# A new order of steps, codes cast by DMAs, and outer-product tables in a two-layer block kernel

## The chip, the core and the metric

One core of a Trainium2 chip runs the program. The time is that of one execution in device microseconds, smaller is better; the median of three runs of the kernel before is 320.33 us (320.06 to 322.46). TensorE (PE) multiplies matrices into eight banks of PSUM; VectorE (DVE), ScalarE (ACT) and GpSimd (POOL) work on tiles; SyncE (SP) issues DMAs. Each engine goes through its own queue in program order and waits on semaphores.

## What is computed

1,024 tokens of width 512 (four sequences of 256) go through two layers, each a normalization and two branches that are added to the input. Cut to what matters:

```python
xn = layernorm(x)                                   # layer 0
h = xn @ Win.T + bin                                # width 64
for l in range(4):
    y = silu(layernorm(h, ln1))
    h = h + scl * real(conv(y, p ** t))             # complex recurrence over a sequence
    y = layernorm(h, ln2)
    h = h + silu(y @ W1.T + b1) @ W2.T + b2
attn = layernorm(h) @ Wout.T + bout
ffn = (silu(xn @ (gate_t * gate_s).T) * (xn @ (up_t * up_s).T)) @ (down_t * down_s).T   # codes -1, 0, 1; width 1792
x = x + attn + ffn
xn = layernorm(x)                                   # layer 1
attn = xn @ (weight * blockmask).T + bias
ffn = low-rank gated layer: U1, V1 (1376 wide), U2, V2
x = x + attn + ffn
```

## The kernel before

The tokens are two blocks `b` of 512, each four tiles `t` of 128. `build_order` makes one list of steps, and every engine walks this list and does its share of each step; so a place in the list is a place in all queues. The backbone are dense steps: `gate` and `up` of 14 column blocks `f` (8 matmuls of 512 columns each: high and low half of the tokens, `xh` and `xl`, times the codes, lines 628 and 629), then 16 `down` quarters (line 723) for each block. In layer 1 follow `u1`, eleven `hidden` pieces, `attn` and `out`. Each dense step is a slot, and small steps are put behind a slot.

The small steps are: `stats`, `root`, `norm`, `xt` (statistics on DVE, the inverse root on POOL at line 1104, the scaled tile XN on DVE at line 927, its transpose on PE at line 590, the copies xh and XT on ACT, the low half `xl` on DVE at line 933); the chain of the 64-wide branch, for each block `win`, and for each depth `t1`, `scan`, `z`, `scale`, `t3`, `low`, `w1`, `w2`, each with a small normalization `ln` that goes PE, ACT (square, line 830), DVE (sum and variance, lines 970 and 971), POOL (root), DVE (`scale`, line 981), PE; the `cast` steps. The places come from distances: `CHAIN_START`, and LN_SLOTS, SCAN_SLOTS and the like from step to step.

Codes are int32 in memory. SP loads each 128x512 block of them into one of six places of `stage`, and ACT (line 816, all `down` and some `up`) or DVE (line 1010) casts it to f16. A place is loaded again when its cast is done. `first` is the pair `gate` 0, `up` 0, done tile by tile as the tokens come; pair 1 waits for all four tiles. Gated products go ACT silu (line 857), DVE `hid` (line 1041), ACT `hidh` (line 789), POOL `hidl` (line 1162), with three buffers.

The recurrence uses tables `rot` of the powers of a unit complex number, 4 depths by 256 powers. They grow by doubling, eight `grow` steps of four instructions (lines 528 and 530): six on POOL, two on DVE, and then `lower` copies half of them (line 964).

The lines that place the sequence of casts read:

```python
after[up_at(0, f) - 1].append(("cast", "gate", f + 2))
after[up_at(0, f)].append(("cast", "up", f + 2))
after[up_at(0, f)].append(("cast", "down", f))
```

## Time and profile before

| | |
|---|---|
| median of the runs | 320.33 us |
| the profiled execution, and its span | 320.86 us, 319.0 us |
| PE, PEld busy | 289.1, 188.6 us |
| DVE, ACT, POOL busy | 203.1, 127.6, 151.8 us |
| PE waits for DVE `XN`, in total | 13.5 us in 4 waits |
| PE waits for DVE `lno`, `ymini`, `hid` | 3.6, 3.1, 2.1 us |
| chain that ended last: PE, DVE, POOL | 68%, 15%, 7% |
| loads of codes, 42 of 256 KB, issue to landing | 2.9 to 3.1 us |

Usual instructions: the ACT copy of a transposed tile 0.60 us, the ACT cast 0.62, silu 0.69, DVE `xl` 0.69, tile statistics 0.69 + 0.18 + 0.15, XN 0.55, `hid` 0.75, the DVE cast of codes 0.43, DVE sums of squares 0.42, `scale` 0.69, a 128x256 product on DVE 0.42, the centring of `rows` and `win` 19.24 to 22.40 us, POOL `hidl` 1.16 to 1.47.

The span goes from the first to the last instruction. Matmul ends are modelled, so a matmul's length says less than the time from start to start. Idle time of an engine matters where another waits for it.

### The profile page before, as it was taken

The numbers are of one execution on the slowest core, as the hardware profiler recorded it, in microseconds if no ns is written. First come the engines' busy times: TensorE is split into PE (matmuls) and PEld (weight loads), VectorE is DVE, ScalarE is ACT, GpSimd is POOL, SyncE is SP. The second block draws the span as 40 slices with busy tenths as digits, with TensorE's granted clock in tenths as the row PEclk, the third lists the DMA queues.
The fourth block names the chain that finished last, engine by engine and source line by source line (L and its number), as shares of the span: only waits on it lengthen the run. The fifth ranks groups of instructions, "written<-read, shape, count | busy, mean of one in ns | idle before, by whom it ended". The sixth has DMA issues, their size and how long they took to land.

```text
span 319.0 us, 4327 instructions
## 1 busy us (share of the span) xinstructions
PE 289.1 (91%) x1514; PEld 188.6 (59%) x1514; DVE 203.1 (64%) x316; ACT 127.6 (40%) x213; POOL 151.8 (48%) x161
## 2 busy tenths in 40 slices
PE   0859596989999999999999999996999999999995
PEld 0737253746456564656456464553658888888784
DVE  3679899998764758556675654578977751333313
ACT  1563363555663313254553626212114671045610
POOL 3476452869625220236534444616066893029920
PEclk9999798999999999999999999999999999999999
DMA  7947333645531001301010011110001000110003
GB/s 215 325 150 260 104 106 93 197 129 170 165 132 35 6 26 35 99 0 47 7 33 20 33 35 34 35 31 2 1 8 61 0 0 2 66 66 2 0 1 132
DMA packets 12261, 22.84 MB, mean 72 GB/s; under 512 B 1360, under 2 KB 1872, under 8 KB 12240
## 3 DMA queue, kind: packets, MB, share of 16 engines
q1 hardware_dynamic: 12240, 22.57, 22.2%
q8 instruction: 12, 0.20, 0.2%
q14 instruction: 9, 0.07, 0.1%
HBM read 20.46 MB, written 2.10 MB: 71 GB/s over the span
## 4 chain that ended last, share of the span: by engine, by line
PE 68%; DVE 15%; POOL 7%; issue 4%; ACT 3%; DMA 1%; SPq 0%; DVEq 0%; ACTq 0%; POOLq 0%
PE bank L723 11%; PE bank L628 9%; PE bank L629 9%; PE bank L598 8%; PE bank L596 8%; PE bank L597 8%; PE bank L683 4%; POOL root L1104 3%; PE bank L590 2%; POOL hidl L1162 2%; DVE uscan L999 2%; PE bank L661 2%; POOL X L1150 2%; PE bank L655 1%; DMA X<-in_x 1%
## 5 line engine op out<-in xcount | busy, mean ns | idle before, releaser
L1162 POOL TENSOR_TENSOR hidl<-hid,hidh 128x512 f16<-128x512 f32 x28 | 34.0, 1214 | 62.5 <-ACT hidh L789 62.5
L628 PE MATMUL bank<-xh,upw 128*128 128x512 f16 (+1 forms) x124 | 44.7, 371 | 2.4 <-DVE hid L1041 2.1
L628 PE MATMUL bank<-xh,gatew 128*128 128x512 f16 (+1 forms) x124 | 44.7, 371 | 1.7 <-DVE xl L933 1.4
L629 PE MATMUL bank<-xl,upw 128*128 128x512 f16 (+1 forms) x124 | 44.8, 371 | 0.0
L629 PE MATMUL bank<-xl,gatew 128*128 128x512 f16 (+1 forms) x124 | 44.5, 369 | 0.0
L723 PE MATMUL bank<-downw,hidh 128*128 128x512 f16 x112 | 42.5, 379 | 0.0
L723 PE MATMUL bank<-downw,hidl 128*128 128x512 f16 x112 | 42.4, 379 | 0.0
L1104 POOL TENSOR_TENSOR root<-var,powers 128x4 f32<-128x4 f32 (+1 forms) x25 | 24.9, 996 | 35.1 <-DVE var L971 26.4
L1168 POOL TENSOR_TENSOR actl<-hid,acth 128x512 fp32r<-128x512 f32 (+1 forms) x22 | 28.4, 1300 | 22.7 <-ACT acth L796 22.2
L857 ACT ACTIVATE silu<-bank,early 128x512 f32<-128x512 f32 x28 | 19.2, 687 | 32.3 <-PE bank L629 32.3
L1041 DVE SCALAR_TENSOR_TENSOR hid<-bank,early,silu 128x512 f32<-128x512 f32 x28 | 21.0, 750 | 13.9 <-PE bank L629 13.0
L1072 DVE SCALAR_TENSOR_TENSOR hid<-bank,early,silu 128x512 f32<-128x512 f32 (+1 forms) x22 | 16.5, 750 | 17.8 <-ACT silu L872 14.5
L872 ACT ACTIVATE silu<-bank,early 128x512 f32<-128x512 f32 (+1 forms) x22 | 15.1, 688 | 26.6 <-PE bank L598 26.6
L590 PE MATMUL bank<-early,XN 128*128 128x128 f32 x64 | 11.9, 319 | 13.5 <-DVE XN L927 13.5
L628 PEld LDWEIGHTS bank<-xh,upw 128*128 128x128 f16 x124 | 13.0, 105 | 15.0 <-DVE hid L1041 2.6
L970 DVE TENSOR_REDUCE ssum<-lno 128x4 f32<-128x256 f32 x18 | 7.6, 420 | 21.6 <-ACT lno L830 21.4
L628 PEld LDWEIGHTS bank<-xh,gatew 128*128 128x128 f16 x124 | 13.0, 105 | 13.9 <-DVE xl L933 1.9
L789 ACT ACTIVATE hidh<-hid 128x512 f16<-128x512 f32 x28 | 17.4, 622 | 7.9 <-DVE hid L1041 7.9
L830 ACT ACTIVATE lno<-bank 128x256 f32<-128x256 f32 x18 | 6.9, 381 | 34.2 <-PE bank L683 18.3
L629 PEld LDWEIGHTS bank<-xl,upw 128*128 128x128 f16 x124 | 12.7, 102 | 11.2 <-issue 0.7
L629 PEld LDWEIGHTS bank<-xl,gatew 128*128 128x128 f16 x124 | 12.7, 102 | 10.9 <-issue 0.5
L590 PEld LDWEIGHTS bank<-early,XN 128*128 128x128 f32 x64 | 9.2, 166 | 16.7 <-issue 14.4
(145 smaller groups left out, 640.4 us busy)
## 6 DMA issues: line engine op xcount, KB each, us to landing
stage<-in_gate SPq DMA_DIRECT2D x14, 256.0 KB, 3.1
stage<-in_up SPq DMA_DIRECT2D x14, 256.0 KB, 2.9
stage<-in_down SPq DMA_DIRECT2D x14, 256.0 KB, 2.9
X<-in_x SPq DMA_DIRECT2D x8, 256.0 KB, 6.5
out_x<-X SPq DMA_DIRECT2D x8, 256.0 KB, 2.0
stage<-in_v SPq DMA_DIRECT2D x6, 256.0 KB, 2.6
stage<-in_mask SPq DMA_DIRECT2D x4, 256.0 KB, 3.0
stage<-in_weight SPq DMA_DIRECT2D x4, 256.0 KB, 2.6
```

The source lines that it names most:

```text
L590: mm = pe.transpose(bank_of(key)[:, k * P:(k + 1) * P], XN[:, key[2], k * P:(k + 1) * P], ident)
L596: pe.matmul(dst, lhs[0], rhs[0], start=first, stop=False)
L597: pe.matmul(dst, lhs[0], rhs[1], start=False, stop=False)
L598: return pe.matmul(dst, lhs[1], rhs[0], start=False, stop=last)
L628: pe.matmul(bank_of(key)[:, c], w, xh[b][:, k, c], start=(k == 0), stop=False)
L629: mm = pe.matmul(bank_of(key)[:, c], w, xl[b][:, k, c], start=False, stop=(k == KT - 1))
L723: mm = pe.matmul(bank_of(key)[:], part[:, f, t * P:(t + 1) * P], codes["down"][:, f, :], start=(f == 0 and part is hidh), stop=(f == FT - ...
L857: act.activation(silu[:, n % UNITS, :], bank_of(step)[:], ACT.Silu, scale=col("gate_s", f)).then_inc(silu_ready, 1)
L1041: emit(dve.scalar_tensor_tensor(out=hid[:, n % UNITS, :], in0=bank_of(step)[:], scalar=col("up_s", f), in1=silu[:, n % UNITS, :], op0=ALU. ...
L1104: pool.tensor_tensor(root[i][:, t:t + n], var[i][:, t:t + n], powers[:, 0, t:t + n], ALU.pow).then_inc(root_ready[i], 1)
L1162: pool.tensor_tensor(hidl[:, n % FT, :], hid[:, n % UNITS, :], hidh[:, n % FT, :], ALU.subtract).then_inc(hid_lo, 1)
L1168: pool.tensor_tensor(actl[0:K, n % UNITS, :], hid[0:K, n % UNITS, :], acth[0:K, n % UNITS, :].bitcast(F32), ALU.subtract).then_inc(hid_lo, 1)
```

## The change

The order becomes a table: each small step has a slot of its own, with decimals for its rank within the slot (`LN_AT`, `CHAIN_AT` and so on), and the prologue is written out as `PROLOGUE`. The dense steps keep their order but for `attn` and `u1` in layer 1.

- Only `gate` and `up` 0 and 1 go through `stage` and are cast by ACT. All other codes are loaded by six DMAs of POOL that cast from int32 to f16 on the way, straight into the code tiles; PE waits for the semaphore of the whole load. `stage` has five places. SP's queue is shorter by 38 loads; `early` is loaded by ACT's queue.
- The first two pairs are done tile by tile; four banks hold them, and transposes of tiles 2 and 3 take the two banks of `h`.
- The tables: POOL makes 16 fine and 16 coarse powers (eight `grow` steps of three instructions), `turn` copies them to `turned`, and each depth's table is an outer product, two multiplications and an addition of 128x256: depth 0 on DVE, 1 to 3 on POOL.
- The copy XT is a step of its own, `xcopy`, and the bank of a transpose is free only behind it; `xl` reads the bank and no longer XT.
- The square goes to a tile `sq` with a column for epsilon, and one reduction makes the variance.
- `u1` writes its low half to a tile of its own, `plow`. The casts of `w` no longer wait for the last `wo`. ACT loads its silu table at the start. WARM is 0: PE does nothing ahead of the first tokens, as before.

```diff
-NSTAGE = 6
+FIRST_LOADS = 4
+NSTAGE = 5
...
-CHAIN_START = (3, 12)
-LN_SLOTS, SCAN_SLOTS = 2, 3.3
...
+PROLOGUE = ((("seed", 0), ("stats", 0), ("stats", 1), ("norm", 0), ("seed", 1), ("norm", 1), ("stats", 2)),
+            (("xt", 0), ("codes", 0), ("load", 0), ("norm", 2), ("seed", 2), ("stats", 3), ("grow", 0)),
+            (("xt", 1), ("codes", 1), ("first", 0, 0), ("norm", 3), ("load", 1), ("grow", 1)),
+            (("xt", 2), ("first", 0, 1), ("xcopy", 0), ("first", 1, 0), ("grow", 2), ("grow", 3)),
+            (("xt", 3), ("first", 1, 1), ("xcopy", 1), ("first", 2, 0), ("first", 2, 1), ("xcopy", 2),
+             ("first", 3, 0), ("first", 3, 1), ("xcopy", 3)))
+EARLY_GROWTHS = 4
+WARM = 0
...
+CODE_LOADS = (("gate", 2, 6), ("up", 2, 6), ("gate", 6, 14), ("up", 6, 14), ("down", 0, 7), ("down", 7, 14))
+LOAD_AT = (0.2, 0, 7.1, 16.2)
+GROW_AT = (0, 0, 0.1, 0.5, 0.5, 0.5)
+LN_AT = (0.1, 1.1, 1.2, 1.4, 1.7, 4.1, 4.4, 5.0, 6.4)
+TABLE_AT = (5.3, 7.8, 8.1, 13.3)
+XT_AT = (4.5, 6.6, 8.9, 9.3)
+XCOPY_AT = (7.5, 8.0, 9.1, 9.9)
...
-def cast_by_act(kind, i):
-
-    return kind == "down" or i == 0 or (kind == "up" and 1 < i < ACT_UPS)
...
+        if kind == "xt" and step[1] == 0 and step[2] >= 2:
+            take(step, RING + step[2] - 2)
...
-        ph, pl = xs
+        ph, pl = xs[0], plow[:]
...
-                "xt": lambda: (xt_hi, at),
+                "xt": lambda: (xt_copied, at),
...
+            for i, (kind, first, end) in enumerate(CODE_LOADS):
+                if kind == cast[0] and first <= cast[1] < end:
+                    eng.wait_ge(codes_in[i], 16)
...
-        def growth(eng, i, part):
-
-
-
-            n = 1 << i
-            known, grown, other = rot[:, :, :, 1:n + 1], rot[:, :, :, n + 1:2 * n + 1], rot_t[:, :, :, 0:n]
-            if part < 2:
-                nth = rot[:, :, part:part + 1, n:n + 1].to_broadcast([P, DEPTH, 2, n])
-                return eng.tensor_tensor(other if part else grown, known, nth, ALU.mult)
-            c = part - 2
-            return eng.tensor_tensor(grown[:, :, c, :], grown[:, :, c, :], other[:, :, 1 - c, :],
-                                     ALU.add if c else ALU.subtract)
...
+        def outer(eng, l, part, work):
+
+
+
+            n = [P, ROOTN, ROOTN]
+            dst = rot[:, l, :].rearrange("p (a c) -> p a c", a=ROOTN)
+            tmp_ = rot_t[:, work, :].rearrange("p (a c) -> p a c", a=ROOTN)
+            if part == 2:
+                return eng.tensor_tensor(dst, dst, tmp_, ALU.add)
+            return eng.tensor_tensor(tmp_ if part else dst, turned[:, part, l, :].unsqueeze(2).to_broadcast(n),
...
-                            for by in codes_ready:
-                                pe.wait_ge(codes_ready[by], len(ternary[by]))
...
+            act.dma_start(early[:], params).then_inc(prm_in, 16)
+            act.wait_ge(pool_chain, 1)
+            act.activation(warm[:], powers[:, 0, 0:1], ACT.Silu)
...
-                    if b == 1 and t == 0:
-                        act.wait_ge(h_full[0], 1)
-                        act.wait_ge(xt_lo, TPB)
                     wait_full(act, step)
                     src = bank_of(step)[:].rearrange("p (k n) -> p k n", k=KT)
                     c = slice(t * P, (t + 1) * P)
-                    act.activation(xh[b][:, :, c], src, ACT.Copy)
-                    act.activation(XT[:, :, c], src, ACT.Copy).then_inc(xt_hi, 1)
+                    act.activation(xh[b][:, :, c], src, ACT.Copy).then_inc(xt_hi, 1)
+                elif kind == "xcopy":
+                    _, b, t = step
+                    if b == 1 and t == 0:
+                        act.wait_ge(h_full[0], 1)
+                    act.wait_ge(xt_lo, b * TPB + t + 1)
+                    src = bank_of(("xt", b, t))[:].rearrange("p (k n) -> p k n", k=KT)
+                    act.activation(XT[:, :, t * P:(t + 1) * P], src, ACT.Copy).then_inc(xt_copied, 1)
...
-                    act.activation(lno[b][:, :, 0:DIM], h[b], ACT.Square).then_inc(sq_ready[b], 1)
+                    act.activation(sq[b][:, :, 0:DIM], h[b], ACT.Square, scale=DIM ** -0.5).then_inc(sq_ready[b], 1)
...
-                    emit(dve.tensor_reduce(ssum[b][:], lno[b][:, :, 0:DIM], AX.X, ALU.add))
-                    emit(dve.tensor_scalar(var[b][:], ssum[b][:], 1.0 / DIM, EPS, ALU.mult, ALU.add),
-                         var_ready[b])
+                    emit(dve.tensor_reduce(var[b][:], sq[b][:], AX.X, ALU.add), var_ready[b])
...
-                            if i == 0:
-                                wait_full(dve, ("wo", 1, TPB - 1))
...
+                    half, i = divmod(step[1], GROWTHS // 2)
+                    table, n = (fine, coarse)[half], 1 << i
+                    if half == 1 and i == 0:
+                        link(pool.tensor_copy(coarse[:, :, 1, :], fine[:, :, ROOTN, :]))
+                    both = [P, DEPTH, 2, 2 * n]
+                    known = table[:, :, 1:n + 1, :].rearrange("p l t c -> p l (t c)").unsqueeze(2).to_broadcast(both)
+                    nth = table[:, :, n, :].unsqueeze(3).to_broadcast(both)
+                    link(pool.tensor_tensor(prod[:, :, :, 0:n, :].rearrange("p l a t c -> p l a (t c)"),
+                                            known, nth, ALU.mult))
+                    link(pool.tensor_tensor(table[:, :, n + 1:2 * n + 1, 0], prod[:, :, 0, 0:n, 0],
+                                            prod[:, :, 1, 0:n, 1], ALU.subtract))
+                    link(pool.tensor_tensor(table[:, :, n + 1:2 * n + 1, 1], prod[:, :, 0, 0:n, 1],
+                                            prod[:, :, 1, 0:n, 0], ALU.add))
...
+                elif kind == "table" and step[1] > 0:
+
+                    for part in range(2):
+                        link(outer(pool, step[1], part, 1))
+                    outer(pool, step[1], 2, 1).then_inc(table_ready, 1)
+                    pool.wait_ge(table_ready, step[1])
+                elif kind == "load":
+                    what, first, end = CODE_LOADS[step[1]]
+                    pool.dma_start(codes[what][:, first:end, :],
+                                   source[what][first:end].rearrange("f p d -> p f d")).then_inc(
+                                       codes_in[step[1]], 16)
```

**VectorE, behind the last `xl` of the prologue.** `hid` is the gated product of a pair, `st`, `mv`, `var` the statistics of a tile of the second block, `gatew` a cast, `rot` and `yff` the growth of the tables, XN the scaled tiles. Before:

```order
L1010 CAST gatew<-stage 128x512
L911 BN_STATS st<-X 128x6
L912 BN_AGGR mv<-st 128x2
L1041 SCALAR_TENSOR_TENSOR hid<-bank,early,silu 128x512
L911 BN_STATS st<-X 128x6
L912 BN_AGGR mv<-st 128x2
L911 BN_STATS st<-X 128x6
L912 BN_AGGR mv<-st 128x2
L915 TENSOR_SCALAR var<-mv 128x4
L528 TENSOR_TENSOR rot<-rot 128x8x64
L528 TENSOR_TENSOR yff<-rot 128x8x64
L530 TENSOR_TENSOR rot<-rot,yff 128x4x64 x2
```

After:

```order
L1011 SCALAR_TENSOR_TENSOR hid<-bank,early,silu 128x512
L885 BN_STATS st<-X 128x6
L886 BN_AGGR mv<-st 128x2
L885 BN_STATS st<-X 128x6
L886 BN_AGGR mv<-st 128x2
L885 BN_STATS st<-X 128x6
L886 BN_AGGR mv<-st 128x2
L889 TENSOR_SCALAR var<-mv 128x4
L942 TENSOR_REDUCE var<-sq 128x4
L1011 SCALAR_TENSOR_TENSOR hid<-bank,early,silu 128x512
L901 TENSOR_SCALAR XN<-X,mv,root 128x512 x2
L908 TENSOR_TENSOR xl<-bank,xh 128x4x128
```

The `hid` of the upper list is that of pair 1; the lower list begins with pair 0, and pair 1 is its tenth row. The casts among the statistics and the growth behind the variance are gone; `hid` 1 stands behind all statistics and behind the first sum of squares (`var<-sq`), where it stood in their middle.

**GpSimd, from the last growth to the first `hidl` and roots.** Before:

```order
L528 TENSOR_TENSOR rot<-rot 128x8x32
L528 TENSOR_TENSOR yff<-rot 128x8x32
L530 TENSOR_TENSOR rot<-rot,yff 128x4x32 x2
L1162 TENSOR_TENSOR hidl<-hid,hidh 128x512 x2
L1104 TENSOR_TENSOR root<-var,powers 128x4 x2
L1162 TENSOR_TENSOR hidl<-hid,hidh 128x512
L1183 TENSOR_TENSOR W1l<-stage,W1h 128x512
L1162 TENSOR_TENSOR hidl<-hid,hidh 128x512
```

After, where the casting loads stand between growth instructions (two places), and then the end of the tables:

```order
L1120 TENSOR_TENSOR fine<-prod 128x4x8
L1137 DMA upw<-in_up 128x8x512
L1112 COPY coarse<-fine 128x4x2
L1116 TENSOR_TENSOR prod<-coarse 128x8x2
```

```order
L1120 TENSOR_TENSOR coarse<-prod 128x4x4
L1137 DMA gatew<-in_gate 128x8x512
L1116 TENSOR_TENSOR prod<-coarse 128x128
```

```order
L1124 COPY turned<-coarse 64x64
L1125 TENSOR_SCALAR turned<-coarse 64x64
L1126 COPY turned<-coarse 64x64
L1127 COPY turned<-coarse 64x64
L1162 TENSOR_TENSOR hidl<-hid,hidh 128x512
L1079 TENSOR_TENSOR root<-var,powers 128x4 x2
L1162 TENSOR_TENSOR hidl<-hid,hidh 128x512 x2
L1183 TENSOR_TENSOR W1l<-stage,W1h 128x512
L1162 TENSOR_TENSOR hidl<-hid,hidh 128x512
L1137 DMA downw<-in_down 128x7x512
L497 TENSOR_TENSOR rot<-turned,fine 128x256
L497 TENSOR_TENSOR rot_t<-turned,fine 128x256
```

Four DMAs of POOL have come in ahead of the first `hidl`, two of them with 128x8x512 elements; the 128x256 growth is gone, `turned` has come, and the tables of depths 1 and 2 follow behind the third `hidl`, with the load of `down`.

**SyncE, behind the prologue's loads.** Before:

```order
L567 DMA tmp<-in_rows 128x320
L568 DMA late<-in_params 128x960
L570 DMA X<-in_x 128x512 x4
L561 DMA stage<-in_gate 128x512
L561 DMA stage<-in_up 128x512
L561 DMA stage<-in_down 128x512
```

After:

```order
L532 DMA tmp<-in_rows 128x320
L533 DMA late<-in_params 128x960
L535 DMA X<-in_x 128x512 x4
L526 DMA stage<-in_wide 128x512
L538 DMA bc<-in_rows 128x1024
L526 DMA stage<-in_wide 128x512 x2
L526 DMA stage<-in_mask 128x512 x4
```

The loads of codes are gone from it; what is left goes through five places.

## Rows read from the trace of the kernel before

**Rows 1.** Stages: stretch, its us, busy us (instructions) of PE, PEld, DVE, ACT, POOL, clock, DMA.

```profile
25.50:62.10 36.60, 29.56 (x167) 18.71 (x166) 34.37 (x50) 14.80 (x27) 18.46 (x19) 0.91 0.46 144
62.10:120.00 57.90, 56.27 (x310) 32.59 (x310) 40.33 (x61) 26.91 (x46) 29.16 (x24) 1.00 0.31 98
120.00:200.00 80.00, 78.03 (x426) 45.04 (x425) 49.73 (x76) 36.43 (x60) 31.35 (x28) 1.00 0.12 34
200.00:233.00 33.00, 29.68 (x152) 17.55 (x150) 26.41 (x45) 5.59 (x9) 12.66 (x11) 1.00 0.06 17
233.00:315.60 82.60, 82.60 (x370) 65.36 (x368) 35.57 (x52) 31.68 (x52) 45.52 (x37) 1.00 0.06 21
```

**Rows 2.** Timeline of PE: start us, us, engine, line, what [idle before <-releaser].

```profile
7.94 1.08 PE L590 MATMUL bank<-early,XN 128*128 128x128 f32 x4 [7.94 <-DVE XN L927]
...
11.08 0.31 PE L629 MATMUL bank<-xl,gatew 128*128 128x128 f16 x1
11.19 0.31 PE L628 MATMUL bank<-xh,gatew 128*128 128x128 f16 x1
...
23.70 0.39 PE L628 MATMUL bank<-xh,upw 128*128 128x512 f16 x1 [2.06 <-DVE hid L1041]
...
25.22 0.38 PE L629 MATMUL bank<-xl,upw 128*128 128x512 f16 x1
...
36.57 1.09 PE L590 MATMUL bank<-early,XN 128*128 128x128 f32 x4 [3.88 <-DVE XN L927]
...
51.99 1.10 PE L661 MATMUL bank<-late,ymini 128*128 128x64 f32 x8 [3.05 <-DVE ymini L1002]
...
58.62 3.68 PE L646 MATMUL bank<-late,XT 128*128 128x64 f32 x32
62.14 0.38 PE L628 MATMUL bank<-xh,upw 128*128 128x512 f16 x1
...
223.18 0.47 PE L693 MATMUL bank<-Wouth,xs 128*128 128x512 f32 x1 [1.61 <-issue]
```

**Rows 3.** Stages as in rows 1, the two behind the long pauses.

```profile
36.20:39.60 3.40, 3.03 (x10) 1.62 (x11) 2.63 (x4) 1.08 (x2) 0.00 (x0) 0.50 0.35 131
53.30:56.70 3.40, 3.40 (x12) 1.70 (x10) 3.23 (x6) 1.42 (x3) 0.75 (x1) 0.50 0.27 84
```

**Rows 4.** 17.5 to 61.6 us of lines 1010, 528, 530 alone (two: DVE, then POOL).

```profile
17.50:61.60 44.10, 6.34 (x11) 0.92 0.45 142
...
17.50:61.60 44.10, 4.61 (x4) 4.74 (x12) 0.92 0.45 142
...
17.50:61.60 44.10, 2.54 (x4) 3.59 (x12) 0.92 0.45 142
```

**Rows 5.** Timeline of DVE, columns as in rows 2.

```profile
6.11 0.69 DVE L911 BATCH_NORM_STATS2 st<-X 128x6 f32<-128x512 f32 x1 [1.54 <-DMA X<-in_x]
...
40.42 0.43 DVE L1010 CAST gatew<-stage 128x512 f16<-128x512 int32 x1
...
42.07 1.39 DVE L1029 CAST W1h<-stage 128x512 fp32r<-128x512 f32 x1
```

**Rows 6.** 18.8 to 28.9 us of POOL alone, the growth of before.

```profile
18.80:28.90 10.10, 8.22 (x24) 1.00 0.59 170
```

**Rows 7.** Timeline of POOL.

```profile
4.71 1.02 POOL L1117 TENSOR_TENSOR pz<-pz,powers 128x4 f32<-128x4 f32 x1
...
28.96 1.16 POOL L1162 TENSOR_TENSOR hidl<-hid,hidh 128x512 f16<-128x512 f32 x1
...
33.39 2.66 POOL L1104 TENSOR_TENSOR root<-var,powers 128x4 f32<-128x4 f32 x2
```

**Rows 8.** Timeline of SP's own DMA queue.

```profile
3.04 0.43 SPq L561 DMA_DIRECT2D stage<-in_gate  x1
```

**Rows 9.** Stage in which the loads run densest; last two: DMA share, GB/s.

```profile
12.00:14.00 2.00, 1.67 (x13) 1.62 (x13) 1.88 (x4) 0.31 (x1) 1.68 (x4) 1.00 1.04 404
```

More of the change, by code:

```diff
@@ L85, with dense_order @@
 U2_CHUNKS = chunks_of(IT * RANK)
[L88 to L116 removed]
+def dense_order():
+    dense = []
@@ new lines, in dense_order, with chain, norm_big @@
+    return dense
+def chain(b):
+    jobs = [[("win", b), ("ln", b)], [("scale", b)]]
+    for l in range(DEPTH):
+        jobs += [[("t1", b, l)], [("scan", b, l)], [("z", b, l), ("ln", b)], [("scale", b)], [("t3", b, l)],
+                 [("low", b)], [("w1", b, l)], [("w2", b, l), ("ln", b)], [("scale", b)]]
+    return jobs + [[("tf", b)], [("low", b)], [("wo", b, 0), ("wo", b, 1)], [("wo", b, 2), ("wo", b, 3)]]
+def norm_big(layer, b):
+    return ([[("stats", layer, b, t)] for t in range(TPB)] + [[("root", layer, b, 0, TPB)]]
+            + [[("norm", layer, b, t)] for t in range(TPB)])
@@ L302, in two_layers @@
     casts = [s[1:] for s in order if s[0] == "cast"]
-    ternary = {e: [c for c in casts if c[0] in ("gate", "up", "down") and (cast_by_act(*c) == (e == "act"))]
+    ternary = {e: [c for c in casts if c[0] in ("gate", "up") and e == "act"]
                for e in ("act", "dve")}
@@ L630, in gate_up @@
                 return mm
+            pe.wait_ge(ones_ready, 1)
+            for _ in range(WARM):
+                pe.matmul(banks[0][:], onesr[:], onesr[:, 0:1].to_broadcast([P, D]), start=True, stop=True)
             pe.wait_ge(prm_in, 16)
```

325 lines of the change are left out of this document (143 added, 182 removed).

## The prediction

> **What bounds the kernel now.** I read the page's engine shares first: TensorE is busy 289.1 of 319.0 us, so it carries the kernel and all that can be won is its idle time and its slow time. A table of stages then says where that lies. From 233.0 to 315.6 us it is never idle; from 62.1 to 233 it idles 1.63 + 1.97 + 3.32 = 6.9 us in short pieces; behind the last matmul come 3.4 us of adding and storing [rows 1]. From 25.5 to 62.1 it is idle 36.6 - 29.6 = 7.0 us [rows 1]. Before its first instruction stand 7.94 us, and the pieces behind it are seen one by one in its timeline: 2.06 us before the second `up` block, 3.88 us before the transpose at 36.57 (waiting for VectorE's normalized tile) and 3.05 us before `z` at 51.99 (waiting for the scan on VectorE) [rows 2]. Behind each of the two long pauses the granted clock reads 0.50 for 3.4 us, that is 1.2 in place of 2.4 GHz [rows 3]; behind the 2.06 us pause 128x512 matmuls go on at (25.22 - 23.70)/7 = 0.22 us from start to start, which is full speed [rows 2]. Two stretches of 3.4 us at half speed cost up to 1.7 us each.
>
> In the same stretch VectorE is nearly full: 34.4 of 36.6 us [rows 1]. So early on VectorE's queue sets the pace, and from 62 us on TensorE does. My mark for the early part is the start of `up` block 6 behind the second `win`: 62.14 us [rows 2].
>
> **Part 1, VectorE's load.** Between 17.5 and 61.6 us VectorE casts codes 11 times (6.34 us) and grows the tables (4.61 + 2.54 us) [rows 4]: 13.5 us. All of it goes. What comes are three 256-element products for table 0, at 0.42 each (the duration of the 128x256 `rot` instructions of before), 1.3 us; the `TENSOR_SCALAR` behind each block's sum of squares also goes. If VectorE alone set the pace, the mark would move up about 12 us.
>
> **Part 2, the first tokens, walked.** The walk takes its durations from the trace (the table of usual instructions above has those without a row): a transposed tile 1.1 us at the low clock and 0.45 at the high, 16 matmuls of 128 columns at 0.11 us each [rows 2] cold = 1.7 and 0.9 warm, copies 0.6, `xl` 0.7, statistics of a tile 1.1, normalization 0.55. Normalized tile 0 waits behind the statistics of tile 1, whose X lands at 6.11 [rows 5]; the parameters no longer stand ahead of it in SP's queue, worth at most the 0.4 us that one issue takes [rows 8]. The first transpose thus comes at 7.4 (7.94 before). TensorE then does tile 0 of pair 0 at 10.5, tile 1 of pair 0 and tile 0 of pair 1 until 16.4, tile 3's transpose at 16.8, and the rest of both pairs until 21.2. Before, pair 1 ended at 25.4 [rows 2]. The number of columns is the same: 64 matmuls of 128 in place of 16 of 512. Splitting is not free where the clock is low, but these are waits anyway.
>
> `win` needs the centred rows and weights: 3.0 us on VectorE behind `xl` of tile 3 and one tile's statistics, so it runs 22.2 to 26.0. `hid` 0 is made at 22.9, then three statistics, the variance and `hid` 1 until 27.7. Next in VectorE's queue stands the normalization of the second block, which needs GpSimd's root.
>
> **Part 3, GpSimd, the term I am least sure of.** Ahead of `hidl` 0 and that root GpSimd now has, behind the last root of the prologue at 13.1: 24 growth instructions and a copy. The 24 of before took 10.1 us with their gaps for larger outputs [rows 6]; the smaller ones I put at 9.2. Four for `scan`, 1.9; four for `turned`, 1.2; three DMA issues. One more issue stands before the prologue's last root. Behind these stand `hidl`, 1.2, and the root, which two of them in 2.66 bound by 1.3; I use 1.3 and 1.0 [rows 7].
> An issue by GpSimd has no row here. Low bound: SP's issue, 0.43 us [rows 8]. High bound: SP's 0.43 for 128 rows of 2 KB scaled by the rows, 1.7 for 512 and 3.4 for 1,024. I take 1.0, nearer to the low one, since SP's own issue does not show a price by row. The power of eight columns costs 1.0 to 2.0, from 1.02 for four [rows 7]; I take 1.65, which the walk holds. Sum: 13.1 + 9.2 + 1.9 + 1.2 + 3.0 = 28.4, root at 30.7. VectorE is ready at 27.7 and waits 3.0 us; TensorE, done with `gate` 2 at 27.5, waits 3.2 us for the transpose.
>
> From there: `up` 2 to 32.9, `gate` 3, second transpose, `up` 3 to 36.8, `t1` to 37.3, a wait of 1.4 us for ScalarE's late copy of XT (the bank of the first transpose is freed only by it, and it is queued behind `t1`'s `ymini`), `gate` 4, two transposes, `up` 4, `gate` 5 to 44.8. The scan is ready by 43, so `z` no longer waits. `up` 5, `gate` 6, `win` until 52.6. The pause of 3.2 us is like the 3.05 us one that let the clock fall [rows 2, 3]: I add 1.0 (0 to 1.7). The mark is at 53.6: **8.5 us** gained. Bounds: with TensorE never waiting behind 21.2, its work up to the mark is 26.3 us (two `win` at 3.8, nine blocks at 1.73, four transposes and `t1` at 0.45, `z` 0.84), so 47.5 and 14.6 us gained; with the dear issues (0.7 + 5.5 us more) 59.8 and 2.3 us.
>
> **Part 4, after the mark.** Of the 6.9 us the pieces of 0.56 us stand before `t1` and `t3`, whose `scale` waits behind GpSimd's 1.2 us `hidl`; the largest, 1.61 us, before `Wout` at 223.18 [rows 2]. The new table gives the links more room, 3 to 5 places from `z` to `t3` where all had 3, the reduction makes the variance itself, and VectorE loses two or three casts in the 62 to 120 us stretch. I leave 1.5 us: **5.4 us** gained, bounds 0.5 and 6.6. The later `u1` of block 1 has a copy and a subtraction (1.5 us) under 1.4 us of `out`: 0.1. The first hidden pieces lose the `attn` between them, but four pieces at 1.43 us cover the 3.6 us from gate to `actl`. TensorE's work, 289 us, does not change: in the stretch without idle nothing can be won. ScalarE's casts go too; its queue was no bound, since it is idle more than half of the time in each stage from 25.5 us on [rows 1].
>
> Sum: 319.0 - 8.5 - 5.4 = 305.1 us of span. The profiled execution took 320.86 for a span of 319.0, so 1.86 around it: 307.0; the median of the runs shown is 0.5 lower, so **306.4 us**.
>
> **A rule against this change.** VectorE's casts and GpSimd's work disturb each other here: a 128x512 cast takes 0.43 alone, and one of the same size took 1.39 while GpSimd was in a `hidl` [rows 5]. If an issue waits for one such cast, that is 0.4 us each, 1.3 us for three: the sum would be 307.7. The Trainium skill ("SBUF — State Buffer", the "DVE blocks DMA" trap) says that a DMA issued from GpSimd is starved of descriptors while VectorE runs a two-port instruction. By that rule 307.7 would be the better number; no run here shows a load issued by GpSimd. The new prologue leaves VectorE a single cast between 13 and 28 us, that of the rows, so I keep the sum.
>
> **Rivals.**
> - *Forecast* (0.50): the sum, 303.5 to 309.5.
> - *TensorE hardly waits* (0.22): an issue costs 0.4 and GpSimd is ready when VectorE is; mark at 48 to 50, 0.5 to 1 us idle later: 319.0 - 13.1 - 6.1 + 1.3 = 301.1 (1.3 from span to median).
> - *Issues hold GpSimd long* (0.13): 3.4 us for the large ones. Mark at 59.8, and 4.5 us idle later, since the late loads for `down` stand in the same queue: 319.0 - 2.3 - 2.4 + 1.3 = 315.6.
> - *New waits eat the gain* (0.07): the late XT copies, the stage with five places in place of six, and the masked weights, which make GpSimd wait for a landing, bring new gaps of some 10 us: 316 to 322, no change.
> - *Slower: the casting transfers are slow* (0.08). Each load has one semaphore, so `gate` 6 waits for the whole 2 MB, and 6 MB must have landed before `up` 6. Issued from 10 us on, they may last until 61 without making the mark later than before: 6 MB in 51 us, 123 GB/s. Plain loads run at 404 GB/s here [rows 9], and 3.3 times slower is what it takes. At 75 GB/s they end at about 94: 319 + 32 = 351 us. For it: no row shows a casting transfer. Against it: the margin.
>
> **How the numbers follow.** Over 1% faster is below 317.1: forecast, TensorE hardly waits, long issues, and a little of the new waits: 0.86. Within 1%: 0.06. Slower: 0.08. (1% is about what a measurement of this kernel tells from no change.) The range, 300.5 to 315, takes the first two cases and the lower part of the third; left out are its upper part (0.04) and the last two, 0.19 in all.
>
> **What would show it.** The first transpose at 7.4 and the second pair's last 128-column matmul near 21; VectorE waiting for `root` before the second block's `XN` near 28; GpSimd's time between the prologue's last root and the first `hidl`, 15.3 us; `z` of block 0 without a wait; `up` 6 at 53.6; idle of TensorE behind it under 2 us. I am wrong if loads land after 25.5 (TensorE waiting for DMA), or if idle behind the mark stays at 7 us.

## The result, and the profile after

The changed kernel takes 305.9 us (median of four runs, 305.4 to 307.0) beside 320.2 us for the kernel before, timed with it: a ratio of 0.954, 95% interval 0.949 to 0.959. 306.4 us was predicted, with 300.5 to 315 as the range. The profiled execution took 306.1 us with a span of 304.2, against 319.0 before.

Stages of the changed kernel, columns as in [rows 1]; the first goes from the end of the first `win` to the mark, the start of `up` 6:

```profile
24.90:54.60 29.70, 24.29 (x136) 14.37 (x136) 19.34 (x28) 11.58 (x21) 18.91 (x26) 0.94 0.65 113
54.60:112.00 57.40, 57.40 (x321) 33.99 (x319) 34.75 (x47) 23.83 (x39) 33.61 (x29) 1.00 0.16 31
112.00:192.00 80.00, 80.00 (x436) 46.43 (x434) 46.40 (x68) 37.07 (x61) 36.23 (x33) 1.00 0.10 28
192.00:225.00 33.00, 32.22 (x165) 19.34 (x165) 27.53 (x50) 5.65 (x11) 11.43 (x11) 1.00 0.11 36
225.00:304.20 79.20, 75.73 (x337) 60.99 (x335) 31.22 (x44) 30.38 (x50) 41.92 (x33) 1.00 0.08 29
```

Set beside [rows 1], VectorE is no longer full in the first stage (19.3 of 29.7 us, where it was 34.4 of 36.6), and behind the mark TensorE idles 0.8 us, where it idled 6.9. (The 3.5 us in the last stage are the adding and storing behind the last matmul, as before.) TensorE's timeline, columns as in [rows 2]; these are all of its rows with a wait:

```profile
7.31 1.94 PE L555 MATMUL bank<-early,XN 128*128 128x128 f32 x8 [7.31 <-DVE XN L901]
9.94 0.29 PE L593 MATMUL bank<-xh,gatew 128*128 128x128 f16 x1 [0.70 <-DVE xl L908]
...
20.07 0.22 PE L594 MATMUL bank<-xl,upw 128*128 128x128 f16 x1
21.19 0.36 PE L584 MATMUL bank<-rowhl,onesr 128*128 128x256 f32 x1 [0.90 <-DVE late L871]
...
24.90 0.38 PE L593 MATMUL bank<-xh,gatew 128*128 128x512 f16 x1
...
30.84 0.63 PE L555 MATMUL bank<-early,XN 128*128 128x128 f32 x4 [4.05 <-DVE XN L901]
...
40.56 0.39 PE L593 MATMUL bank<-xh,gatew 128*128 128x512 f16 x1 [1.36 <-ACT XT L785]
...
46.63 1.00 PE L630 MATMUL bank<-late,ymini 128*128 128x64 f32 x8
...
54.55 0.38 PE L593 MATMUL bank<-xh,upw 128*128 128x512 f16 x1
...
201.85 0.63 PE L624 MATMUL bank<-early,lno 128*128 128x128 f32 x4 [0.78 <-DVE lno L951]
```

The mark fell from 62.14 [rows 2] to 54.55, 7.6 us, and from the mark to the end the span fell from 256.9 to 249.65, 7.2 us. Together that is the 14.8 us by which the span fell (the medians differ by 14.3). The 3.05 us wait before `z` [rows 2] is gone; one pause of 4.05 us is left. The chain that ended last shows what made it (start, us, what; the longest pieces of its early part):

```profile
9.67 1.12 POOL gatew L1137
13.89 0.84 POOL upw L1137
18.04 0.96 POOL upw L1137
22.72 0.95 POOL gatew L1137
27.48 1.15 POOL hidl L1162
28.64 1.02 POOL root L1079
```

GpSimd's four issues of casting loads (the DMAs that turn int32 codes into f16 on the way; the issue is the time for which GpSimd is held), then `hidl` 0, then the root that the second block's normalization waits for. VectorE's timeline has the other end of it, where XN waits for that root:

```profile
26.07 0.75 DVE L1011 SCALAR_TENSOR_TENSOR hid<-bank,early,silu 128x512 f32<-128x512 f32 x1
30.15 1.89 DVE L901 TENSOR_SCALAR XN<-X,mv,root 128x512 f32<-128x512 f32 x2 [3.33 <-POOL root L1079]
```

### The profile page after: what moved, and what is told of

It reads as the page before. It is cut to its first block, busy times and chain, and to the rows that moved or that the text cites. A ratio compares the mean times of both kernels' runs of the same rounds, so it can differ in the third digit from the quotient of the medians.

```text
span 304.2 us, 4356 instructions
## 1 busy us (share of the span) xinstructions
PE 285.6 (94%) x1562; PEld 190.5 (63%) x1562; DVE 175.6 (58%) x270; ACT 118.4 (39%) x197; POOL 159.5 (52%) x184
## 4 chain that ended last, share of the span: by engine, by line
PE 85%; POOL 6%; DVE 4%; issue 2%; DMA 1%; ACT 1%; DVEq 0%; POOLq 0%
PE bank L593 15%; PE bank L594 15%; PE bank L690 14%; PE bank L561 8%; PE bank L563 8%; PE bank L562 8%; PE bank L652 5%; PE bank L624 3%; PE bank L630 2%; PE bank L555 2%; PE bank L642 1%; PE bank L643 1%; DMA early<-in_params 1%; PE bank L615 1%; POOL root L1079 1%
## 5 line engine op out<-in xcount | busy, mean ns | idle before, releaser
L594 PE MATMUL bank<-xl,upw 128*128 128x512 f16 (+1 forms) x136 | 45.7, 354 | 0.0
L1079 POOL TENSOR_TENSOR root<-var,powers 128x4 f32<-128x4 f32 (+1 forms) x25 | 23.6, 948 | 23.5 <-DVE var L942 19.8
L593 PEld LDWEIGHTS bank<-xh,gatew 128*128 128x128 f16 x136 | 14.0, 103 | 13.8 <-ACT XT L785 1.6
L845 ACT ACTIVATE silu<-bank,early 128x512 f32<-128x512 f32 (+1 forms) x22 | 15.1, 687 | 19.0 <-PE bank L563 18.8
L593 PEld LDWEIGHTS bank<-xh,upw 128*128 128x128 f16 x136 | 14.2, 105 | 11.8 <-issue 1.1
L555 PE MATMUL bank<-early,XN 128*128 128x128 f32 x64 | 10.7, 301 | 11.4 <-DVE XN L901 11.4
L594 PEld LDWEIGHTS bank<-xl,upw 128*128 128x128 f16 x136 | 13.9, 102 | 11.5 <-issue 0.8
L594 PEld LDWEIGHTS bank<-xl,gatew 128*128 128x128 f16 x136 | 13.9, 102 | 10.8 <-issue 0.3
L942 DVE TENSOR_REDUCE var<-sq 128x4 f32<-128x260 f32 x18 | 7.6, 424 | 20.4 <-ACT sq L803 20.3
L690 PEld LDWEIGHTS bank<-downw,hidh 128*128 128x128 f16 x112 | 11.2, 100 | 12.8 <-issue 1.6
L561 PE MATMUL bank<-xs,V1h 128*128 128x512 f32 (+1 forms) x44 | 18.0, 409 | 0.1
## 6 DMA issues: line engine op xcount, KB each, us to landing
upw<-in_up POOLq DMA_DIRECT2D x1, 1024.0 KB, 12.1
```

The source lines that it names most:

```text
L561: pe.matmul(dst, lhs[0], rhs[0], start=first, stop=False)
L593: pe.matmul(bank_of(key)[:, c], w, xh[b][:, k, c], start=(k == 0), stop=False)
L594: mm = pe.matmul(bank_of(key)[:, c], w, xl[b][:, k, c], start=False, stop=(k == KT - 1))
L690: mm = pe.matmul(bank_of(key)[:], part[:, f, t * P:(t + 1) * P], codes["down"][:, f, :], start=(f == 0 and part is hidh), stop=(f == FT - ...
L1079: pool.tensor_tensor(root[i][:, t:t + n], var[i][:, t:t + n], powers[:, 0, t:t + n], ALU.pow).then_inc(root_ready[i], 1)
```

## The experiments

Twelve kernels ran; each ratio is to the kernel before in the same batch, whose median went from 320.2 to 321.6 us. The changed kernel was timed in a batch of its own, so a difference from it reads a little otherwise by the ratios than by the medians; below, both are given where it matters. Spans and marks are those of the profiled executions.

| kernel | median us | ratio to before | 95% interval | span | mark |
|---|---|---|---|---|---|
| changed kernel | 305.9 | 0.954 | 0.949 to 0.959 | 304.2 | 54.55 |
| root_first | 303.0 | 0.943 | 0.940 to 0.946 | 301.6 | 51.97 |
| old_chain | 311.0 | 0.969 | 0.964 to 0.973 | 308.2 | 52.43 |
| casts_back | 309.8 | 0.963 | 0.959 to 0.967 | 306.6 | 54.85 |
| first_one | 305.8 | 0.951 | 0.948 to 0.954 | 304.0 | 54.36 |
| split_loads | 308.3 | 0.960 | 0.958 to 0.963 | 306.8 | 57.11 |
| xcopy_early | 304.9 | 0.951 | 0.948 to 0.953 | 302.9 | 53.26 |
| warm12 | 305.9 | 0.953 | 0.951 to 0.955 | 303.5 | 53.84 |
| root_xcopy_table | 302.6, again 302.5 | 0.943, 0.943 | 0.941 to 0.944 | 300.9, 300.6 | 51.24, 50.98 |
| scan_early | 306.6 | 0.955 | 0.950 to 0.960 | 305.2 | 50.10 |
| before_room | 318.0 | 0.993 | 0.990 to 0.995 | 316.0 | 61.05 |
| scan_w1 | 308.0 | 0.960 | 0.957 to 0.962 | 306.3 | 48.08 |

**GpSimd's queue.** Does it set the long pause? root_first puts the last growth step, the four `scan` products and the four `turned` copies behind the root (3.8 us of GpSimd's time in the changed kernel), and the load of `gate` 6 to 13 behind the first `hidl`:

```diff
-LOAD_AT = (0.2, 0, 7.1, 16.2)
-GROW_AT = (0, 0, 0.1, 0.5, 0.5, 0.5)
+LOAD_AT = (1.3, 0, 7.1, 16.2)
+GROW_AT = (0, 0, 0.1, 2.5, 2.5, 2.5)
```

> Only the order of GpSimd's queue changes, against the changed kernel (305.9 us): the last growth, the four scan products and the four `turned` copies go behind the roots of the second block, and the load of `gate` 6 to 13 goes behind the first `hidl`. Theory (GpSimd's queue sets the 4.05 us pause of TensorE at 30.84): the statistics of the block are ready at 24.9, the root at about 26.0, XN behind `hid` 1 at 26.8, the transpose at 27.5; the pause is 1 us and the granted clock does not fall, so the kernel gains 3.3 + 1.5 us: about 301, and the two levels of the clock show by whether the gain is 3 or 5. Rival (the pause would only move, because the scan on VectorE at 43.0 or the copies of XT then hold the next steps): less than 1.5 us gained, with a new wait before `z` or `gate` 4.

303.0 us, 2.9 us faster (3.6 by the ratios), where about 301 was expected. The root began at 25.67 and TensorE's pause shrank to 0.77 us; the granted clock stayed at 1.00. What was not expected is the first of these two waits; the second was there before:

```profile
35.99 0.63 PE L624 MATMUL bank<-early,lno 128*128 128x128 f32 x4 [1.52 <-DVE lno L951]
...
37.98 0.39 PE L593 MATMUL bank<-xh,gatew 128*128 128x512 f16 x1 [1.36 <-ACT XT L785]
```

VectorE's and then GpSimd's timeline of the same kernel say why `lno` was late:

```profile
32.08 1.26 DVE L497 TENSOR_TENSOR rot<-turned,fine 128x256 f32<-128x256 f32 x1
33.27 0.41 DVE L497 TENSOR_TENSOR rot_t<-turned,fine 128x256 f32<-128x256 f32 x1
33.72 1.40 DVE L496 TENSOR_TENSOR rot<-rot,rot_t 128x256 f32<-128x256 f32 x1
```

```profile
31.83 1.23 POOL L1162 TENSOR_TENSOR hidl<-hid,hidh 128x512 f16<-128x512 f32 x1
33.69 1.15 POOL L1162 TENSOR_TENSOR hidl<-hid,hidh 128x512 f16<-128x512 f32 x1 [0.63 <-ACT hidh L756]
```

Of three equal products of table 0, the two that met a `hidl` took 1.26 and 1.40 us, the one between them 0.41; both long ones ended 0.28 us behind the `hidl` beside them. In the changed kernel, with GpSimd idle, they took 0.42 or 0.43. So the theory on the pause holds; but the growth behind the root held `hidl` 1 back (31.83 for 30.60) until VectorE made its table.

**The price of an issue.** split_loads makes two issues of each casting load, each with half of the rows (both on the load's semaphore, whose waits go from 16 to 32):

```diff
-                    pool.dma_start(codes[what][:, first:end, :],
-                                   source[what][first:end].rearrange("f p d -> p f d")).then_inc(
-                                       codes_in[step[1]], 16)
+                    mid = (first + end) // 2
+                    for a, z in ((first, mid), (mid, end)):
+                        pool.dma_start(codes[what][:, a:z, :],
+                                       source[what][a:z].rearrange("f p d -> p f d")).then_inc(
+                                           codes_in[step[1]], 16)
```

> The changed kernel (305.9 us) with each of the six casting loads issued in two halves, so twelve issues of 256 or 512 rows (448 for `down`). Four of the added issues... of the six added, one stands ahead of the prologue's last root and three behind it ahead of the root of the second block. Theory (an issue costs GpSimd about 0.95 us whatever its rows, 0.84 to 1.14 in the changed kernel, and its queue sets XN of the second block): each half costs 0.9 to 1, the XN comes 3 to 4 us later than 30.8, the kernel takes 309 to 310. Rival A (the cost goes with the rows): a half costs 0.5, nothing changes, 305.5 to 306.5. Rival B (GpSimd's queue doesn't set it): issues at 1 us each and still 306.

308.3 us, 2.4 us slower. GpSimd's timeline, two issues in a row, 2 x 256 rows and then 2 x 512, and the root behind them:

```profile
14.18 1.53 POOL L1139 DMA_DIRECT2D upw<-in_up  x2 [0.30 <-POOL fine L1120]
19.15 1.55 POOL L1139 DMA_DIRECT2D upw<-in_up  x2 [0.30 <-POOL fine L1120]
...
30.44 2.14 POOL L1079 TENSOR_TENSOR root<-var,powers 128x4 f32<-128x4 f32 x2
```

A half costs 0.77 us with 256 rows as with 512, where the whole had cost 0.84 and 0.96: mostly fixed, hardly by row. The root came 1.85 us later (30.44 for 28.59), TensorE's transpose 1.84 us later, and the mark 2.6. Rivals A and B both fall; my 0.95 for a half was too much.

No issue of the changed kernel took more than 1.14 us. That longest one, the first, has 512 rows like the 0.84 us one, and it alone has an XN of VectorE (a `TENSOR_SCALAR`) beside it:

```profile
9.92 0.55 DVE L901 TENSOR_SCALAR XN<-X,mv,root 128x512 f32<-128x512 f32 x1
```

The issue, 9.66 to 10.80, ended 0.33 us behind it. In warm12 the XN ended 0.14 us sooner after the start of the issue; the issue took 1.01 us and again ended 0.34 us behind it. So this issue looks held back by up to 0.3 us, though no run takes the XN away. The three issues that stand ahead of the second block's root have no XN or cast beside them and took 0.84 to 0.96. The Trainium skill ("SBUF — State Buffer", "SBUF: two separate sides") has the "DVE blocks DMA" trap: a DMA issued from GpSimd is starved of descriptors while VectorE runs a two-port instruction. The first issue agrees with it; whether that XN runs in the two-port form no row shows. By the rule the prediction had 307.7, with three issues that each wait for a cast; none of the three met one, so that price was not paid here and is not disproved either. The Trainium skill, in the same section, says that VectorE and GpSimd share a pair of ports that one instruction holds to its end, and that what wants it meanwhile waits: the 1.26 and 1.40 us products agree.

**Casts by DMAs.** casts_back undoes them alone: no casting loads, the other 38 blocks through `stage`, cast as before by VectorE and ScalarE.

```diff
-CODE_LOADS = (("gate", 2, 6), ("up", 2, 6), ("gate", 6, 14), ("up", 6, 14), ("down", 0, 7), ("down", 7, 14))
+CODE_LOADS = ()
+ACT_UPS = 6
...
-    place(LOAD_AT, [[("load", i)] for i in range(2, len(CODE_LOADS))])
+    for f in range(FT):
+        if f + 2 < FT:
+            after[2 * f].append((2 * f, [("cast", "gate", f + 2)]))
+            after[2 * f + 1].append((2 * f + 1, [("cast", "up", f + 2)]))
+        after[2 * f + 1].append((2 * f + 1, [("cast", "down", f)]))
```

> The changed kernel with the DMAs' casts undone: the six casting loads of GpSimd go, SyncE loads the other 38 blocks of codes through `stage` (five places), and VectorE and ScalarE cast them as in the kernel before, at the same places; order, tables and the tile-by-tile pairs stay. Theory (VectorE's load matters early, the casts are 6.3 of its 13.5 us saved): GpSimd comes 3 to 4 us earlier to the root, VectorE has 6 us more up to the mark, and the mark falls 2 to 6 us later than 54.6: 308 to 312 us. Rival (VectorE was not the bound any more and the issues cost GpSimd as much as the casts cost VectorE): 304.5 to 307. A third, five places for 46 loads are too few, so that TensorE waits for loads: over 315.

309.8 us: the DMAs' casts are worth 3.9 us by the medians, 2.8 by the ratios, 2.4 by the spans. VectorE had 20 casts of codes, 13.2 us in all, and GpSimd, free of four issues, came to the root at 25.39 in place of 28.59. TensorE had no pause before the second block's transpose (29.47 for 30.84), in part because its clock was at half from about 23.5 to 30.3; it waited 0.78 for `z`, 1.55 before the second `win` and 1.05 for `lno` at 62.97. The two costs nearly cancel up to the mark (54.85 for 54.55), where 2 to 6 us later was expected; behind it casts_back loses 2.1 us. So the time fell into the theory's range, 308 to 312, but not by the theory's way.

**First pairs, and warming.** first_one leaves pair 1 whole; warm12 sets WARM to 12.

```diff
-FIRST = 2
+FIRST = 1
...
-WARM = 0
+WARM = 12
```

(In first_one the `first` steps of pair 1 also leave `PROLOGUE`.)

> The changed kernel with only pair 0 done tile by tile, pair 1 behind it in 128x512 matmuls, as in the kernel before. By the walk, pair 1 (64 matmuls of 128 columns) filled waits for tokens up to 21.2; undone, TensorE waits there and does 3.5 us of matmuls behind the last tile: `win` 2 to 3 us later. Theory A (that stretch sets the pace): 307.5 to 309. Theory B (GpSimd's queue and its root at 30.7 set the pace behind it, so up to 4 us of delay before it are free): 305.5 to 306.5, the 4.05 us pause shorter by what `win` is later.

> The changed kernel with WARM at 12: twelve 128x512 products of a constant tile ahead of the first tokens, whose result is overwritten. Theory (the first pairs wait for tokens, and GpSimd's root at 30.7 sets what follows): TensorE's granted clock or pitch is full at 7.3 in place of 14.4, pairs end a little earlier, and the time stays at 305.4 to 306.6. Rival (the low clock early on is on the path): 1 to 2 us faster. A third, 12 products last beyond 7.3 us: up to 1 us slower.

305.8 and 305.9 us: neither gains anything that the medians show. In first_one the pause before the transpose was 2.65 us in place of 4.05, and the transpose came at 30.64, where it was: what the tile-by-tile pair saved ended in the wait for GpSimd. In warm12 the twelve products stood from 1.04 to 6.29 at 0.44 us each, and the tokens came at 7.26 no earlier. The first 128-column matmuls still went at 0.107 us (9.80, 9.91, 10.02), with the granted clock now reading 0.50 there; the full pitch came at 12.77 in place of 14.49, and that too went into the wait for GpSimd. A second stretch at half clock, from about 23 to 33, lasted past the transpose at 30.47, so warm12 does not show the warming alone.

**Room in the order.** old_chain puts the 64-wide branch at the distances of before (2 from `z` to `scale`, 1 to `t1` and `t3`, and so on) behind `z` of block 0 and from the second `win`; before_room is the kernel before with the changed places for the links from `scale` behind `z` of block 0 to its last `w2`, and from `scale` of block 1; within a slot the order of before stays.

```diff
-CHAIN_AT = ((2.0, 5.6, 7.3, 8.8, 10.0, 11.4, 13.1, 13.6, 15.3, 18.3, 20.5, 21.4, 21.9, 25.6, 27.7, 30.7, 30.9, 32.2, 33.7, 36.6, 37.6, 38.5, 42.3, 43.2, 45.2, 46.3, 47.8, 50.7, 51.5, 55.0, 55.0, 58.4, 59.3, 61.7, 62.3, 64.4, 66.1, 70.9, 71.0, 72.8, 74.4, 75.1), ...
+CHAIN_AT = ((2.0, 5.6, 7.3, 8.8, 10.0, 12.0, 13.0, 14.0, 16.0, 18.6, 20.6, 21.6, 22.6, 25.9, 27.9, 28.9, 29.9, 31.9, 34.5, 36.5, 37.5, 38.5, 41.8, 43.8, 44.8, 45.8, 47.8, 50.4, 52.4, 53.4, 54.4, 57.7, 59.7, 60.7, 61.7, 63.7, 66.3, 68.3, 69.3, 70.3, 72.3, 73.3), ...
```

> Only the places of the 64-wide branch change, against the changed kernel: behind `z` of block 0, and from `win` of block 1 at place 12, the steps stand at the distances of the kernel before (2 from `z` to `scale`, 1 to `t1` and `t3`, 3.3 from scan to `z`). Theory (the room in the table took away the idle time behind the mark): 4 to 6 us of idle come back, in pieces of 0.5 us before `t1` and `t3`; about 311. Rival (the lighter VectorE and the one reduction took it away): under 1.5 us comes back, 306 to 307.

> The kernel before (320.3 us) with one part of the change alone: behind `z` of block 0 up to its last w2, and from `scale` of block 1, the steps of the 64-wide branch stand at the changed kernel's places; codes are still cast by VectorE and ScalarE, tables, reduction and the early order are those of before. In the other direction (old_chain) the places were worth 5.1 us. Theory (the room alone takes the idle time behind the mark away, whatever VectorE's load): 4 to 6 us faster than before, 314.5 to 316.5. Rival (the room helps only where VectorE is lighter): at most 2 us faster, 318.5 or more, with waits for `lno` left behind 62 us.

old_chain takes 311.0 us. Behind the mark its span is 255.8 us, where the changed kernel has 249.65 and the one before 256.9. Its timeline has ten pauses there, 5.6 us in all, nine of them for `lno`. These are the first three:

```profile
58.69 0.63 PE L624 MATMUL bank<-early,lno 128*128 128x128 f32 x4 [0.47 <-DVE lno L951]
76.02 0.63 PE L624 MATMUL bank<-early,lno 128*128 128x128 f32 x4 [0.56 <-DVE lno L951]
90.59 0.63 PE L624 MATMUL bank<-early,lno 128*128 128x128 f32 x4 [0.41 <-DVE lno L951]
```

So nearly all of the gain behind the mark (6.1 of 7.2 us) hangs on the places, though VectorE was lighter and the variance came from one instruction. Yet before_room gains only 2.4 us, between its theory (4 to 6) and its rival (at most 2), and 5.1 us of idle stay behind its mark. With the changed kernel's other parts the places are worth 5.1 us (4.5 by the ratios), with those of before 2.4. That would fit places that help only if the links are as short as the table supposes, but it is argued, not shown. Which of the lighter load, the reduction and the order of other steps makes the difference, no run separates.

**Copies of XT, and a faster kernel.** xcopy_early moves one step, root_xcopy_table adds it and one more to root_first:

```diff
-XCOPY_AT = (7.5, 8.0, 9.1, 9.9)
+XCOPY_AT = (7.2, 8.0, 9.1, 9.9)
...
-TABLE_AT = (5.3, 7.8, 8.1, 13.3)
+TABLE_AT = (5.8, 7.8, 8.1, 13.3)
```

> The changed kernel with one step moved: the first copy XT of block 1 stands ahead of `t1` of block 0 (place 7.2 in place of 7.5). Theory (as predicted, the bank waits only for this copy, queued on ScalarE behind the activation of `t1`): the 1.36 us wait before `gate` 4 goes and the kernel gains 1.0 to 1.4 us, 304.5 to 305. Rival (VectorE's scan or the next transposes hold what follows): the wait moves behind and less than 0.5 us is gained.

> The order of root_first (303.0 us) with two more moves: the first XT copy of block 1 ahead of `t1`, and the three products of table 0 behind `scale` of block 0 on VectorE (place 5.8 in place of 5.3). In root_first the first and third product took 1.26 and 1.40 us beside GpSimd's `hidl` and TensorE waited 1.52 us for `lno`, then 1.36 for XT. Theory (two separate waits): both go, 303.0 - 1.4 - 1.3 = 300.3 us. Rival (with the table later the scan is later, and `z` waits for it): 301 to 302.5 with a wait before `z`.

> The same kernel as root_xcopy_table, beside scan_w1 on one chip, for the comparison of the two: 302.6 us again, `z` waiting 1.9 us. Whether TensorE's granted clock stays at 1.00 throughout in a second profiled execution is open: kernels with the same program up to 36 us fell to 0.5 at 22.7, at 31.5 or not at all.

In xcopy_early the 1.36 us wait went and 1.29 us came before `z`: the wait moved, as the rival had it. Its median, 304.9, is 1.0 us lower, but the executions of the two overlap (304.3 to 306.2, 305.4 to 307.0), and so do the intervals of their ratios; its profiled execution kept the clock at 1.00 behind the pause. root_xcopy_table takes 302.6 us, 0.4 less than root_first, with overlapping intervals: both waits went and 1.93 us before `z` came, as its rival had it. Its median is the lowest found, 3.3 us below the changed kernel's, and its second batch gave 302.5, the profiled execution with the clock at 1.00 again. Two attempts to free `z` started from it and moved the scan of block 0 to place 8.0 and the casts of W1 behind it: scan_early with the W1 casts at 9.3 and 10.6 and GpSimd's tables at 12.2, 14.2 and 17.2, scan_w1 with the casts at 9.6 and 9.8 and the tables at 9.2, 9.5 and 13.3.

> The order of root_xcopy_table (302.6 us) with VectorE's queue ahead of `z` of block 0 emptied: the scan of block 0 at place 8.0 in place of 8.8, the two casts of W1 behind it (9.3 and 10.6), and GpSimd's tables 1 to 3, which slow VectorE beside them, at 12.2, 14.2 and 17.2. In root_xcopy_table `z` waited 1.93 us, and between the ready `ymini` and the scan VectorE did two casts of W1 and one `hid`, 2.0 us. Theory: the scan starts at 36.9 in place of 38.2 and takes 3.9 in place of 4.6 us, `z` waits 0 to 0.3 us, 302.6 - 1.7 = 300.9 us. Rival (tables and W1 now collide with the later links): the gain is under 0.7 us and idle time appears behind the mark.

> Between root_xcopy_table (302.6 us) and scan_early (306.6 us): the scan of block 0 at 8.0 and the two casts of W1 behind it, at 9.6 and 9.8, but GpSimd's tables 1 and 2 only just behind the fourth `hidl`, at 9.2 and 9.5, and table 3 at 13.3 as in the changed kernel. In scan_early TensorE waited 0.90 and 2.55 us for `lno` behind the mark, where GpSimd had a table and then 5.4 us of adding biases ahead of a root. Theory (the moved tables made those waits): they go, `z` waits under 0.5 us, and the kernel takes 301 us, 1.5 faster than root_xcopy_table. Rival (the W1 casts or the early scan made them): 303 to 306 again, with idle time before the second or third `lno`.

`z` was freed (waits of 0.25 and 0.24 us) and both marks came earlier, 50.10 and 48.08 for 51.24, yet both kernels were slower than root_xcopy_table, 306.6 and 308.0. scan_w1's GpSimd, from 37.95 on:

```profile
37.95 1.08 POOL L1137 DMA_DIRECT2D downw<-in_down  x1
45.48 1.15 POOL L1162 TENSOR_TENSOR hidl<-hid,hidh 128x512 f16<-128x512 f32 x1 [6.45 <-ACT hidh L756]
...
51.03 2.48 POOL L1183 TENSOR_TENSOR W1l<-stage,W1h 128x512 fp32r<-128x512 f32 x2
53.47 1.04 POOL L1079 TENSOR_TENSOR root<-var,powers 128x4 f32<-128x4 f32 x1
```

It idled 6.45 us, since the tables now stood behind a `hidl` that was not ready, and then had two tables and two W1 halves ahead of the root. VectorE waited 7.64 us for it and TensorE 5.47 before `lno`, and behind that pause, at a granted clock of 0.50, twelve matmuls of 512 columns started 0.43 us apart in place of 0.22, another 2.5 us. scan_early had the same fault spread over two links (0.90 and 2.55 us); three of its executions took 306.1 to 307.1 us and one, with a mean granted clock of 1.00, 303.7, so part of its loss seems to be the clock. scan_early's rival holds. Of scan_w1's pair neither does as it stands: the two tables (4.4 us) and the two W1 halves (2.5 us) both stood ahead of the root, so the trace does not part the theory's cause from the rival's, and 308.0 lies outside the 303 to 306 of the rival as well.

**The clock.** A granted clock of 1.00 is 2.4 GHz, one of 0.50 is 1.2. The granted clock differed between executions whose programs are the same up to that point. Stages as in [rows 1]: the changed kernel behind its pause, xcopy_early there, and old_chain in and behind its first `win`:

```profile
31.50:34.90 3.40, 3.40 (x9) 1.20 (x8) 1.29 (x3) 0.60 (x1) 0.25 (x1) 0.50 0.94 158
```

```profile
30.80:34.50 3.70, 3.70 (x20) 1.91 (x21) 3.06 (x4) 0.60 (x1) 0.90 (x1) 1.00 0.98 165
```

```profile
22.60:28.60 6.00, 6.00 (x24) 3.89 (x22) 2.58 (x7) 0.38 (x1) 5.11 (x14) 0.51 1.22 221
30.40:34.00 3.60, 3.59 (x19) 1.93 (x20) 3.17 (x4) 0.60 (x1) 1.13 (x1) 1.00 1.16 194
```

In old_chain the half-clock stretch lay in the time for which TensorE would have waited for GpSimd anyway (its pause was 1.35 us), and cost nothing: its mark is 2.1 us earlier than the changed kernel's. The price of the half clock behind the pause is read from the transpose at 30.84 (30.79, 30.41) to the next one, the same work in all three; the changed kernel's, xcopy_early's and old_chain's are:

```profile
36.44 0.60 PE L555 MATMUL bank<-early,XN 128*128 128x128 f32 x4
```

```profile
34.71 0.60 PE L555 MATMUL bank<-early,XN 128*128 128x128 f32 x4
```

```profile
34.32 0.60 PE L555 MATMUL bank<-early,XN 128*128 128x128 f32 x4
```

That is 5.60 us against 3.92 and 3.91: the half clock cost 1.7 us. From the transpose to the mark old_chain, with the same 1.36 us wait, also needs 1.7 us less (22.0 for 23.7).

## Why the prediction was right

The mechanism held: VectorE's queue no longer sets the early pace, GpSimd's does, and the waits behind the mark went with the room in the table, though before_room shows that the room alone does not do it. That the sum came within 0.5 us is in part luck, as the last lines say. Point by point, in its own steps:

- *VectorE's load.* Right: it is busy 65% in the first stage and sets no pace. The 12 us that it alone would have given became 7.6, since GpSimd took over, as Part 3 said.
- *First tokens.* The first transpose came at 7.31 (7.4 predicted), the pairs ended at 20.07 (21.2), `win` started at 21.19 (22.2) and ended at 24.90 (26.0). A microsecond better, and worth nothing, as first_one shows.
- *GpSimd.* From the prologue's last root (ends 12.58) to the first `hidl` (27.48) 14.9 us, 15.3 predicted. The three issues in it were 0.84 to 0.96 (1.0 taken), and each had 0.3 us of idle ahead that I did not count, 3.7 us in place of 3.0; `scan` was 1.2 for 1.9, the growth 8.6 for 9.2, `turned` 1.4 for 1.2. So the root was done at 29.7, a microsecond before the 30.7 of the walk. The transpose still came at 30.84, where 30.7 was predicted, since the walk put nothing between root and transpose: 0.5 us went by until VectorE's XN began at 30.15 (the wait there, 3.33, against 3.0) and 0.7 until the transpose. Two errors of about 1 us cancel there. TensorE waited 4.05 (3.2), because it was done 0.7 us earlier.
- *Clock.* 1.0 taken, 1.7 measured, the upper end of its 0 to 1.7. This is the largest error up to the mark.
- *Waits on the way.* 1.4 for XT, measured 1.36; `z` without a wait, so it was. But xcopy_early shows how little room there was: with the wait for XT gone, `z` waited 1.29 us.
- *The mark.* 53.6 predicted, 54.55 measured: 8.5 and 7.6 us gained. Of the 0.9 us, 0.7 are the clock and 0.1 the later transpose; another 0.1 is the stretch from `z` to the mark, 7.9 us, for which the walk has 7.8 though its own terms (0.84, twice 1.73, 3.8) add up to 8.1.
- *Behind the mark.* 1.5 us of idle left, measured 0.78; the gain was 7.2 us, not 5.4. The matmuls behind the mark are the same in number (1,254 in both traces). Of the 1.8 us, 0.7 are less idle. The other 1.1 are time that the idle column did not show: a row's idle starts at the modelled end of the matmul ahead, 0.38 us long where the next could start after 0.22, so each of the ten pauses of before was longer by up to 0.16. I read 6.9 us as all there was to win. old_chain agrees in size: it has nine pauses more than the changed kernel behind the mark, 4.9 us more of listed idle, and 6.1 us more of time, so 0.14 us more for each pause. No run tests it by itself. The forecast took the room, the reduction and VectorE's lighter load together; old_chain and before_room show that the room is needed for the gain and does not suffice.
- *The rivals.* TensorE hardly waiting: no, though root_first reaches 303.0 by reordering alone. Long issues: no, 0.95 and 0.96 us for 1,024 rows. New waits: the one for XT came and was in the sum. Slow transfers: no. A stage of the changed kernel in which, as far as its rows tell, only casting loads are in flight:

```profile
24.00:28.00 4.00, 2.79 (x18) 1.58 (x17) 2.02 (x5) 1.56 (x3) 3.13 (x12) 1.00 1.24 208
```

208 GB/s as written, in f16; the int32 read is twice that, 416 GB/s, where 123 was the threshold. The list of DMA issues gives 12.1 us from issue to landing for the 512 KB of `gate` 2 to 5, issued at 9.66: there by 21.8, and needed at 24.90.

Two errors of 0.9 us (the mark) and 1.8 us (behind it) with opposite signs make the sum better than its terms, and within the first the early root and the missing XN hide each other. That is luck.
